# Adjacency of a graph network: 400 supersteps of four windows become 200 of eight over two PSUM banks

## The chip, the cores and the metric

The kernel runs on one core of a Trainium2 chip. The metric is the device time of one execution in microseconds (us), the median of several runs.

## The reference

Two graph networks, one after the other, over 3125 nodes and 100000 edges sorted by destination. Each is added to its input and followed by a layer norm. All message passing is a sum over the edges:

```
msg = x[src]
summed = segment_sum(msg, dst, num_segments=3125)
cnt = segment_sum(ones(E), dst, num_segments=3125)
aggr = summed / maximum(cnt, 1.0)[:, None]
out = aggr @ W_l + b_l + x @ W_r
```

The first network does this twice; the second does three layers of aggregation, each with a router that picks two of eight experts. As the edges never change, the kernel counts them once into a dense adjacency matrix in bf16 (how many edges go from source s to destination d) and later multiplies the node features by it.

## The kernel before

The program goes through these parts in order: keys of the edges (to about 124 us), the adjacency matrix (127 to 498 us), its layout into pieces in device memory, two passes of the first network, three layers with experts, and the final projection. Only the adjacency stage and the small tables before it are touched.

**Windows and steps.** A source is split as 25 tiles of 128; a destination belongs to a window of four (`W = 4`). A window of the matrix is therefore `WC = 100` columns on 128 partitions, and there are `NW = 800` of them. The edges come in 800 chunks of 125. A chunk and a window that it touches make a step; there are `T = 1600` steps in the order of the windows. A step is one matmul: a one-hot of the source's low part (125 edges x 128) times a one-hot of the place within the window (125 edges x 100) adds the step's counts to 100 columns of PSUM.

**Supersteps.** `G = 4` steps that follow each other form a superstep, with one PSUM bank. Its windows are at most three beyond its first one. TensorE first clears columns 100 to 399 with a matmul of zeros (L1210), then the first step writes columns 0 to 99 with `start=True`, and each of the other three adds at an offset from its register (L1214). The registers come from `w_rel`, a table of the offsets in the superstep. They are loaded for two batches at once (L1199): 24 registers for eight supersteps.

**Four engines in a chain.** VectorE makes the one-hots of 16 steps, a batch, in two instructions (L702), four batches ahead at most; it waits for `s_step`, which the last matmul of a superstep raises. ScalarE waits for `s_step`, copies the first window to the ring `first_w` of eight places (L1087) and the three others straight into the adjacency matrix (L1089), at an offset from a register. GpSimd adds the first window from the ring to the matrix (L558), because that window can have sums of the superstep before it; it waits for the wide copy (`s_wide`) and its own last add (`s_first`). ScalarE's narrow copy waits until the add of eight supersteps before is done, and TensorE's zeroing matmul until ScalarE has copied the superstep of eight before (L1209). GpSimd and ScalarE load 16 registers for 16 supersteps at a time (`RS`, L551 and L1079). The loops: a head of 64 steps with constant waits, then 24 turns of 64 steps each.

The tables `w_off` and `w_rel` are made by VectorE in three instructions (L688 to L690), after which the stage starts. At its end VectorE and ScalarE wait for the last add and start the layout (L356).

Of the kernel before, what the change touches and what calls it, by code (L numbers as in the profile page):

```python
# [11 lines left out]
EPE = mybir.EngineType.PE  # L12
# [4 lines left out]
P = 128  # L17
# [8 lines left out]
NW = S * P // W  # L26
WC = W * S
T = C + NW
G = 4
B16 = 16  # L30
RS = 16
NOH = 4
TP = 400
ABSENT_DST = 8000
# [42 lines left out]
def build(nc, x, src, dst, Wl0, bl0, Wr0, Wl1, bl1, Wr1, W_in, b_in, router_W, router_b, weak_W, weak_b,  # L77
          strong_W1, strong_b1, strong_W2, strong_b2, conf_W, conf_b, W_out, b_out, out):
    with ExitStack() as ctx:
# [3 lines left out]
        def sem(name):  # L83
            return ctx.enter_context(nc.semaphore(name))
# [4 lines left out]
        psum = ctx.enter_context(nc.psum_tensor("psum", [P, 8, 512], F32))  # L89
# [15 lines left out]
        def carve(shape, dt, rows=P):  # L105
            n = 1
            for k in shape:
                n *= k
            cols = n * (1 if dt == BF16 else 2)
            a = arena[0:rows, used[0]:used[0] + cols]  # L110
            used[0] += cols
            assert used[0] <= 103900, used[0]
            a = a if dt == BF16 else a.bitcast(dt)
            names = "abcd"[:len(shape)]
            if len(shape) > 1:
                a = a.rearrange(f"p ({' '.join(names)}) -> p {' '.join(names)}", **dict(zip(names[1:], shape[1:])))
            return a


        adj = carve([NW * WC], BF16)  # L120
        build_from = used[0]
        ones_b = carve([512], BF16)
        zeros_b = carve([512], BF16)
        iota2 = carve([P, 2], BF16)
        lo_of = carve([T], BF16, CE)
        loc_of = carve([T], BF16, CE)
        w_off = carve([T // G], I32, 1)
        w_rel = carve([T // G * (G - 1)], I32, 1)
        oh1 = carve([NOH, B16 // 2, P, 2], BF16, CE)
        wf = oh1[0:1].rearrange("p b n c z -> p (b n c z)")[:, 0:2 * T].bitcast(F32)  # L130
        first_w = carve([8, WC], BF16)
# [132 lines left out]
        s_wide = sem("new_windows_copied"); s_first = sem("first_window_added"); s_zero = sem("adjacency_zeroed")  # L264
# [54 lines left out]
        def blk(p, b):  # L319

            return (p - 2) * NB + b
# [210 lines left out]
        def _(pool):  # L532
# [17 lines left out]
            def adds(i):  # L550
                _, off = nc.values_load_multi_w_load_instructions(  # L551
                    w_off[0:1, bass.ds(i * RS, RS)], engines=(EPOOL,), min_val=0, max_val=(NW - G) * WC,
                    skip_runtime_bounds_check_because="a window's offset")
                for u in range(RS):
                    pool.wait_ge(s_wide, i * RS + u + 2)
                    pool.wait_ge(s_first, i * RS + u + 1)
                    a = adj[:, bass.ds(off[u], WC)]
                    pool.tensor_tensor(a, first_w[:, u % 8], a, ALU.add).then_inc(s_first, 1)  # L558
            with pool.Fori(0, T // G // RS) as i:
                adds(i)  # L560
# [12 lines left out]
            for l in range(NL):  # L573
                pool.memset(b1v[:, l, 0:NS, 2:FT], 0.0).then_inc(s_prep, 1)
            pool.wait_ge(s_first, T // G + 1)
            pool.wait_ge(s_wide, T // G + 1)
            pool.memset(x_all[:, S - 1], 0.0).then_inc(s_xpad, 1)
# [56 lines left out]
        def _(v):  # L634
# [3 lines left out]
            n = [0]  # L638

            def link(ins):  # L640
                n[0] += 1
                ins.then_inc(s_v, 1)
                v.wait_ge(s_v, n[0])
# [42 lines left out]
                v.nop().then_inc(s_gread, 1)  # L686
            w4 = wf[:, :].rearrange("o (s g) -> o s g", g=G)
            link(v.tensor_scalar(w_off[:, :], w4[:, :, 0], float(WC), None, ALU.mult))  # L688
            link(v.tensor_tensor(w_rel[:, :].rearrange("o (s g) -> o s g", g=G - 1), w4[:, :, 1:G], w4[:, :, 0:1].broadcast_to((1, T // G, G - 1)), ALU.subtract))
            v.tensor_scalar(w_rel[:, :], w_rel[:, :], float(WC), None, ALU.mult).then_inc(s_tab, 1)  # L690
            v.wait_ge(s_zero, 2)
            v.wait_ge(s_tab, 1)

            k = B16 // G
# [370 lines left out]
        def _(act):  # L1065
# [3 lines left out]
            for e in range(NE):  # L1069
                n = CAP // P  # L1070
# [7 lines left out]
            def supersteps(i, head=False):  # L1078
                _, off = nc.values_load_multi_w_load_instructions(  # L1079
                    w_off[0:1, bass.ds(i * RS, RS)], engines=(EACT,), min_val=0, max_val=(NW - G) * WC,  # L1080
                    skip_runtime_bounds_check_because="a window's offset")
                for u in range(RS):
                    act.wait_ge(s_step, i * RS + u + 1)
                    if not head or u >= 8:

                        act.wait_ge(s_first, i * RS + u - 6)
                    act.copy(first_w[:, u % 8], psum[:, u % 8, 0:WC])  # L1087
                    act.wait_ge(s_wide, i * RS + u + 1)
                    act.copy(adj[:, bass.ds(off[u] + WC, (G - 1) * WC)], psum[:, u % 8, WC:G * WC]).then_inc(s_wide, 1)  # L1089
            supersteps(0, head=True)  # L1090
            with act.Fori(1, T // G // RS) as i:
                supersteps(i)
# [55 lines left out]
            for p in range(2, 5):  # L1148
# [9 lines left out]
                for b in range(NB):  # L1158
                    i = blk(p, b)
# [14 lines left out]
        def _(pe):  # L1174
# [17 lines left out]
            k = B16 // G  # L1192
            def supersteps(i, head=False):


                for q in range(NOH):
                    if q % 2 == 0:
                        n = 2 * k * (G - 1)
                        _, rel = nc.values_load_multi_w_load_instructions(  # L1199
                            w_rel[0:1, bass.ds(i * (NOH // 2 * n) + q // 2 * n, n)], engines=(EPE,), min_val=0, max_val=(G - 1) * WC,  # L1200
                            skip_runtime_bounds_check_because="a window's offset in its superstep")
                    pe.wait_ge(s_oh1, i * NOH + q + 1)
                    pe.wait_ge(s_oh2, i * NOH + q + 1)
                    for g in range(k):
                        u = q * k + g
                        bank = psum[:, u % 8]

                        if not head or u >= 8:
                            pe.wait_ge(s_wide, i * (NOH * k) + u - 6)  # L1209
                        pe.matmul(bank[:, WC:G * WC], zeros_b[:, 0:P], zeros_b[:, WC:G * WC], start=True, stop=False, skip_group_check=True)  # L1210
                        for z in range(G):
                            cols = bass.ds(rel[(q % 2 * k + g) * (G - 1) + z - 1], WC) if z else slice(0, WC)
                            n = (g * G + z) // 2
                            mm = pe.matmul(bank[:, cols], oh1[:, q, n, :, z % 2], oh2[:, q, n, :, z % 2],  # L1214
                                           start=(z == 0), stop=(z == G - 1), skip_group_check=True)
                        mm.then_inc(s_step, 1)
            supersteps(0, head=True)
            with pe.Fori(1, T // B16 // NOH) as i:
                supersteps(i)
# [279 lines left out]
```

## Time and profile before

| | |
|---|---|
| median of 3 runs | 2634.7 us (2622.96 to 2635.31) |
| the profiled execution's own time | 2652.03 us |
| its span | 2650.4 us |
| TensorE matmuls busy | 2061.1 us (78%) |
| VectorE / ScalarE / GpSimd busy | 887.1 / 605.0 / 682.1 us |
| adjacency stage, first one-hot to last add | 127 to 498 us |

In the rows, PE is TensorE's matmuls and PEld its weight loads; DVE is VectorE, ACT ScalarE, POOL GpSimd. A name that ends in q (PEldq, POOLq) is the engine's sequencer, whose instructions (register loads, register arithmetic, branches) are not counted as busy. `[0.23 <-ACT ...]` behind a row is the idle time before it and what ended it. L12 is line 12 of the kernel.

### The profile page before, as it was taken

The page shows a single profiled execution, that of the slowest core. Times are in us where ns is not written, and L with a number is a line of the kernel's source. Part 1 is how long each engine was busy: PE and PEld are TensorE (multiplying, and loading weights), DVE is VectorE, ACT ScalarE, POOL GpSimd, SP SyncE. Part 2 cuts the span into 40 slices and gives each one's busy share as a digit, 9 for nine tenths or more (in the row PEclk, how much of TensorE's full clock was granted, in tenths as well). Part 3 has the DMA queues.
Part 4 walks back from the last instruction along what each step waited for, and adds up shares of the span by engine and source line. Part 5 has one row for each costly group of instructions (what it writes and reads, how often), then busy time and mean ns, then how long its engine had stood idle before and what let it go on. Part 6 is the DMA issues. An engine that isn't in the chain of part 4 may idle for free.

```text
span 2650.4 us, 37862 instructions
## 1 busy us (share of the span) xinstructions
PE 2061.1 (78%) x12490; PEld 1567.8 (59%) x12491; DVE 887.1 (33%) x2222; ACT 605.0 (23%) x1548; POOL 682.1 (26%) x821
## 2 busy tenths in 40 slices
PE   2666666239999898699958999699958999699953
PEld 1354444226667666577736776577736776577742
DVE  3476666333333322333332011332332011332334
ACT  0055656610011000223311000233211000233310
POOL 4177676300000033222210122222210122222210
PEclk9667676669999888799978989799978999799985
DMA  9400000495476653122256331122257331122232
GB/s 321 129 1 0 0 0 0 167 372 181 146 205 221 214 183 128 61 65 68 70 217 240 106 114 68 53 72 66 65 202 263 106 116 66 54 68 71 65 133 89
DMA packets 180467, 315.84 MB, mean 119 GB/s; under 512 B 48431, under 2 KB 138853, under 8 KB 180226
## 3 DMA queue, kind: packets, MB, share of 16 engines
q1 hardware_dynamic: 132210, 221.11, 25.4%
q0 software_dynamic: 21392, 65.09, 6.8%
q10 hardware_dynamic: 26752, 28.12, 3.2%
q8 instruction: 74, 1.21, 0.2%
q14 instruction: 39, 0.32, 0.0%
HBM read 198.96 MB, written 115.30 MB: 119 GB/s over the span
## 4 chain that ended last, share of the span: by engine, by line
PE 46%; DMA 16%; issue 13%; POOL 8%; DVE 8%; ACTq 3%; ACT 3%; SPq 1%; POOLq 1%; another core or an unknown queue 0%; DVEq 0%
PE psum L1314 14%; PE psum L1428 13%; DMA arena<-xs_d 10%; POOL arena L558 8%; PE psum L1228 7%; DMA arena<-h_d 4%; ACTq L1071 3%; PE psum L1406 2%; DVE arena L992 2%; PE psum L1391 1%; ACT arena L1089 1%; DMA adj_d<-arena 1%; DVE arena L994 1%; PE psum L1233 1%; PE psum L1417 1%
## 5 line engine op out<-in xcount | busy, mean ns | idle before, releaser
L1314 PE MATMUL psum<-arena 128*128 128x320 bf16 x3750 | 549.1, 310 | 89.0 <-DVE arena L1012 75.2
L1314 PEld LDWEIGHTS psum<-arena 128*128 128x128 bf16 x3750 | 376.9, 101 | 256.1 <-issue 98.3
L1417 PE MATMUL psum<-arena 128*128 128x256 f32 x1536 | 360.9, 389 | 2.1 <-ACT arena L1143 2.0
L619 POOL DMA_INDIRECT y_d<-arena,idx x192 | 202.3, 1054 | 605.0 <-DVE arena L994 596.3
L1428 PE MATMUL psum<-arena 128*128 x1536 | 352.5, 382 | 3.2 <-ACT arena L1146 3.2
L1417 PEld LDWEIGHTS psum<-arena 128*128 128x128 f32 x1536 | 281.3, 193 | 66.6 <-ACT arena L1146 18.6
L1428 PEld LDWEIGHTS psum<-arena 128*128 128x128 f32 x1536 | 284.1, 190 | 44.5 <-issue 6.4
L1146 ACT ACTIVATE arena<-psum,b1c 128x256 f32<-128x256 f32 x384 | 181.8, 473 | 494.0 <-PE psum L1417 493.5
L1228 PE MATMUL psum<-arena 128*128 128x320 bf16 x1500 | 225.1, 302 | 80.8 <-DMA arena<-adj_d 80.8
L558 POOL TENSOR_TENSOR arena<-arena 128x100 bf16 x400 | 257.1, 643 | 118.1 <-ACT arena L1089 64.2
L606 POOL DMA_INDIRECT xs_d<-arena,pos x150 | 144.6, 964 | 524.4 <-DVEq L849 483.3
L702 DVE TENSOR_TENSOR arena<-arena 125x1600 bf16<-125x1600 bf16 x200 | 232.5, 1207 | 120.3 <-PE psum L1214 120.2
L1210 PE MATMUL psum<-arena 128*128 128x300 bf16 x400 | 162.9, 407 | 135.9 <-DVE arena L702 74.3
L992 DVE TENSOR_TENSOR arena<-psum,arena 128x256 f32<-128x256 f32 x192 | 81.5, 425 | 528.2 <-PE psum L1428 528.2
L1228 PEld LDWEIGHTS psum<-arena 128*128 128x128 bf16 x1500 | 148.1, 99 | 139.2 <-DMA arena<-adj_d 81.0
L1214 PE MATMUL psum<-arena 125*128 125x100 bf16 x1600 | 204.5, 266 | 0.0
L1214 PEld LDWEIGHTS psum<-arena 125*128 125x128 bf16 x1600 | 171.3, 131 | 36.0
L1089 ACT CAST arena<-psum 128x300 f32 x400 | 166.0, 415 | 0.0
L1210 PEld LDWEIGHTS psum<-arena 128*128 128x128 bf16 x400 | 45.0, 112 | 164.4 <-ACT arena L1089 123.7
L1406 PE MATMUL psum<-ident,arena 128*128 128x128 f32 x384 | 64.1, 290 | 90.9 <-DMA arena<-xs_d 90.3
L1087 ACT CAST arena<-psum 128x100 bf16<-128x100 f32 x400 | 96.9, 242 | 160.6 <-POOL arena L558 112.1
L1116 ACT COPY arena<-psum 128x384 f32<-128x384 f32 (+1 forms) x50 | 19.1, 428 | 489.7 <-PE psum L1356 488.7
(238 smaller groups left out, 1572.8 us busy)
## 6 DMA issues: line engine op xcount, KB each, us to landing
arena<-adj_d SPq DMA_DIRECT2D x125, 800.0 KB, 6.3
xs_d<-zrow ACTq DMA_DIRECT2D x8, 3432.0 KB, 28.9
arena<-xs_d SPq DMA_DIRECT2D x96, 264.0 KB, 2.8
adj_d<-arena SPq DMA_DIRECT2D x25, 800.0 KB, 7.4
arena<-y_d SPq DMA_DIRECT2D x30, 640.0 KB, 6.1
arena<-h_d SPq DMA_DIRECT2D x25, 640.0 KB, 7.2
h_d<-arena POOLq DMA_DIRECT2D x15, 640.0 KB, 3.7
arena<-x_d SPq DMA_DIRECT2D x20, 320.0 KB, 3.7
```

The source lines that it names most:

```text
L558: pool.tensor_tensor(a, first_w[:, u % 8], a, ALU.add).then_inc(s_first, 1)
L606: pool.indirect_dma_start(xs_d, bass.IndirectOffsetOnAxis(ap=pos[:, k, t:t + 1], axis=0), pay[:, k, t], None).then_inc(a_scat, 16)
L619: pool.indirect_dma_start(y_d, bass.IndirectOffsetOnAxis(ap=idx[:, j % 2, h:h + 1], axis=0), ybuf[:, j % 2, h], None).then_inc(b_sc[j % 2] ...
L702: v.tensor_tensor(oh[:, q], every, key, ALU.is_equal).then_inc(ready, 1)
L1089: act.copy(adj[:, bass.ds(off[u] + WC, (G - 1) * WC)], psum[:, u % 8, WC:G * WC]).then_inc(s_wide, 1)
L1146: act.activation(hid[:, j % 2, f], psum[:, 5 + f % 2, 0:M], ACT.Relu, bias=b1c[:, bass.ds(at_b1[j % LOAD] + f, 1)]).then_inc(b_hidf, 1)
L1210: pe.matmul(bank[:, WC:G * WC], zeros_b[:, 0:P], zeros_b[:, WC:G * WC], start=True, stop=False, skip_group_check=True)
L1214: mm = pe.matmul(bank[:, cols], oh1[:, q, n, :, z % 2], oh2[:, q, n, :, z % 2], start=(z == 0), stop=(z == G - 1), skip_group_check=True)
L1228: mm = pe.matmul(psum[:, h, 0:HN], hs[:, k * SK + s, part, 0:P], half(ring[:, k, s], h), start=(k == 0 and s == 0 and part == 0), stop=(k ...
L1314: mm = pe.matmul(psum[:, q, 0:HN], hs[:, k * SK + s, part, f * P:(f + 1) * P], half(ring[:, k, s], h), start=(k == 0 and s == 0 and part = ...
L1417: mm = pe.matmul(psum[:, 5 + f % 2, 0:M], w1s[:, j % 2, f // 2, kt, f % 2 * P:(f % 2 + 1) * P], xsT[:, j % 2, kt], start=(kt == 0), stop=( ...
L1428: mm = pe.matmul(psum[:, h, 0:H], hid[:, j % 2, f, h * P:(h + 1) * P], w1f[:, bass.ds(at_w2 + f * H, H)], start=(f == 0), stop=(f == FT - 1))
```

## The change

`G` becomes 8: 200 supersteps of eight steps. Eight windows of 100 columns don't fit one bank of 512, so a superstep takes two banks that lie side by side: windows 0 to 4 in the first (`GA = 5`, 500 columns), 5 to 7 in the second. An offset from the sixth window on is raised by `PAD = 12` columns, which VectorE works into `w_rel` with two instructions more than a plain product needs. TensorE has two zeroing matmuls per superstep, of 400 and 300 columns, and the ring of PSUM is four pairs of banks instead of eight banks. The registers of the offsets are loaded once per superstep, seven at a time, behind the waits for the one-hots and ahead of the wait for ScalarE. ScalarE copies 100, 400 and 300 columns per superstep. `RS` becomes 8, so GpSimd and ScalarE load eight registers at a time. The ring `first_w` keeps eight places.

```diff
--- before.py
+++ after.py
@@ -26,9 +26,11 @@
 NW = S * P // W
 WC = W * S
 T = C + NW
-G = 4
+G = 8
 B16 = 16
-RS = 16
+RS = 8
+GA = 512 // WC
+PAD = 512 - GA * WC
 NOH = 4
 TP = 400
 ABSENT_DST = 8000
@@ -686,8 +688,10 @@
                 v.nop().then_inc(s_gread, 1)
             w4 = wf[:, :].rearrange("o (s g) -> o s g", g=G)
             link(v.tensor_scalar(w_off[:, :], w4[:, :, 0], float(WC), None, ALU.mult))
-            link(v.tensor_tensor(w_rel[:, :].rearrange("o (s g) -> o s g", g=G - 1), w4[:, :, 1:G], w4[:, :, 0:1].broadcast_to((1, T // G, G - 1)), ALU.subtract))
-            v.tensor_scalar(w_rel[:, :], w_rel[:, :], float(WC), None, ALU.mult).then_inc(s_tab, 1)
+            rel3 = w_rel[:, :].rearrange("o (s g) -> o s g", g=G - 1)
+            link(v.tensor_tensor(w4[:, :, 1:G], w4[:, :, 1:G], w4[:, :, 0:1].broadcast_to((1, T // G, G - 1)), ALU.subtract))
+            link(v.tensor_scalar(rel3, w4[:, :, 1:G], float(GA), float(PAD), ALU.is_ge, ALU.mult))
+            v.scalar_tensor_tensor(rel3, w4[:, :, 1:G], float(WC), rel3, ALU.mult, ALU.add).then_inc(s_tab, 1)
             v.wait_ge(s_zero, 2)
             v.wait_ge(s_tab, 1)
 
@@ -1084,9 +1088,10 @@
                     if not head or u >= 8:
 
                         act.wait_ge(s_first, i * RS + u - 6)
-                    act.copy(first_w[:, u % 8], psum[:, u % 8, 0:WC])
+                    act.copy(first_w[:, u % 8], psum[:, u % 4 * 2, 0:WC])
                     act.wait_ge(s_wide, i * RS + u + 1)
-                    act.copy(adj[:, bass.ds(off[u] + WC, (G - 1) * WC)], psum[:, u % 8, WC:G * WC]).then_inc(s_wide, 1)
+                    act.copy(adj[:, bass.ds(off[u] + WC, (GA - 1) * WC)], psum[:, u % 4 * 2, WC:GA * WC])
+                    act.copy(adj[:, bass.ds(off[u] + GA * WC, (G - GA) * WC)], psum[:, u % 4 * 2 + 1, 0:(G - GA) * WC]).then_inc(s_wide, 1)
             supersteps(0, head=True)
             with act.Fori(1, T // G // RS) as i:
                 supersteps(i)
@@ -1194,22 +1199,20 @@
 
 
                 for q in range(NOH):
-                    if q % 2 == 0:
-                        n = 2 * k * (G - 1)
-                        _, rel = nc.values_load_multi_w_load_instructions(
-                            w_rel[0:1, bass.ds(i * (NOH // 2 * n) + q // 2 * n, n)], engines=(EPE,), min_val=0, max_val=(G - 1) * WC,
-                            skip_runtime_bounds_check_because="a window's offset in its superstep")
                     pe.wait_ge(s_oh1, i * NOH + q + 1)
                     pe.wait_ge(s_oh2, i * NOH + q + 1)
                     for g in range(k):
                         u = q * k + g
-                        bank = psum[:, u % 8]
-
-                        if not head or u >= 8:
-                            pe.wait_ge(s_wide, i * (NOH * k) + u - 6)
-                        pe.matmul(bank[:, WC:G * WC], zeros_b[:, 0:P], zeros_b[:, WC:G * WC], start=True, stop=False, skip_group_check=True)
+                        bank = psum[:, u % 4 * 2:u % 4 * 2 + 2].rearrange("p b n -> p (b n)")
+                        _, rel = nc.values_load_multi_w_load_instructions(
+                            w_rel[0:1, bass.ds(i * (RS * (G - 1)) + u * (G - 1), G - 1)], engines=(EPE,), min_val=0, max_val=(G - 1) * WC + PAD,
+                            skip_runtime_bounds_check_because="a window's offset in its superstep")
+                        if not head or u >= 4:
+                            pe.wait_ge(s_wide, i * (NOH * k) + u - 2)
+                        pe.matmul(bank[:, WC:GA * WC], zeros_b[:, 0:P], zeros_b[:, WC:GA * WC], start=True, stop=False, skip_group_check=True)
+                        pe.matmul(bank[:, 512:512 + (G - GA) * WC], zeros_b[:, 0:P], zeros_b[:, 0:(G - GA) * WC], start=True, stop=False, skip_group_check=True)
                         for z in range(G):
-                            cols = bass.ds(rel[(q % 2 * k + g) * (G - 1) + z - 1], WC) if z else slice(0, WC)
+                            cols = bass.ds(rel[z - 1], WC) if z else slice(0, WC)
                             n = (g * G + z) // 2
                             mm = pe.matmul(bank[:, cols], oh1[:, q, n, :, z % 2], oh2[:, q, n, :, z % 2],
                                            start=(z == 0), stop=(z == G - 1), skip_group_check=True)
```

## Rows read from the trace of the kernel before

**Rows 1.** Stretch, length, busy (instructions) of PE, PEld, DVE, ACT, POOL; clock, DMA, GB/s.

```profile
127.00:498.30 371.30, 242.62 (x2000) 178.39 (x2000) 232.38 (x200) 221.11 (x800) 257.11 (x401) 0.68 0.00 0
```

**Rows 2.** The chain of work that ended last, stage alone, share by line.

```profile
by line: POOL arena L558 58.7%; issue 16.0%; ACT arena L1089 9.7%; POOLq L558 3.0%; POOLq L555 2.4%; ACT arena L1087 1.9%; DVE arena L702 1.7%; PE psum L1210 1.5%; PE psum L1214 1.5%; POOLq L556 1.4%; ACTq L1083 0.8%; POOLq L551 0.6%; ACTq 
```

**Rows 3.** Waits in the stage: us in total, times, longest.

```profile
DVE arena L702 <- PE psum L1214: 120.2, 87, 2.6
ACT arena L1087 <- POOL arena L558: 112.1, 167, 1.6
```

**Rows 4.** Groups of instructions in the stage: busy us, mean ns, idle before.

```profile
L558 POOL TENSOR_TENSOR arena<-arena 128x100 bf16 x400 | 257.1, 643 | 118.1 <-ACT arena L1089 64.2 <-POOL arena L558 53.9
L1089 ACT CAST arena<-psum 128x300 f32 x400 | 166.0, 415 | 0.0
```

**Rows 5.** Timeline: start us, us, engine, line; adds of GpSimd and VectorE's one-hots.

```profile
307.16 2.31 DVE L702 TENSOR_TENSOR arena<-arena 125x1600 bf16<-125x1600 bf16 x2 [0.33 <-PE psum L1214]
308.61 1.06 POOL L558 TENSOR_TENSOR arena<-arena 128x100 bf16 x1 [0.23 <-POOL arena L558]
310.50 0.35 POOL L558 TENSOR_TENSOR arena<-arena 128x100 bf16 x1 [0.23 <-POOL arena L558]
```

**Rows 6.** Register loads (one source line each): count, ns min/median/max, first and last start.

```profile
L1199 PEldq TENSOR_LOAD <-arena x50: 1613/1617/1802, 126.9 to 484.0; - x50
...
L341 ACTq TENSOR_LOAD <-arena x12: 545/549/774, 1074.0 to 2475.7; - x12
L341 PEldq TENSOR_LOAD <-arena x12: 588/598/1132, 1089.2 to 2482.4; - x12
```

**Rows 7.** Source line 1199 in short windows: its load or register work, start us.

```profile
L1199 PEldq TENSOR_LOAD <-arena x1: 1634/1634/1634, 132.8 to 132.8; - x1
...
L1199 PEldq TENSOR_LOAD <-arena x1: 1627/1627/1627, 138.1 to 138.1; - x1
...
L1199 PEldq FUSED_REGOPS  x1: 46/46/46, 144.0 to 144.0; - x1
```

**Rows 8.** TensorE's loop end (L1218) and register offsets of the steps (L1214).

```profile
L1218 PEldq FUSED_REGOPS  x24: 68/68/73, 137.9 to 477.4; - x24
L1218 PEldq COMPARE_BRANCH  x24: 76/208/242, 150.5 to 490.2; - x24
...
L1214 PEldq FUSED_REGOPS  x1200: 37/46/51, 129.0 to 490.0; - x172
```

**Rows 9.** Timeline of ScalarE: its two copies and the next superstep's first.

```profile
310.31 0.24 ACT L1087 CAST arena<-psum 128x100 bf16<-128x100 f32 x1
310.45 0.41 ACT L1089 CAST arena<-psum 128x300 f32 x1
310.89 0.24 ACT L1087 CAST arena<-psum 128x100 bf16<-128x100 f32 x1
```

**Rows 10.** Timeline of TensorE in the head: first and eighth superstep.

```profile
129.04 0.43 PE L1210 MATMUL psum<-arena 128*128 128x300 bf16 x1 [17.15 <-DVE arena L702]
...
133.10 0.45 PE L1210 MATMUL psum<-arena 128*128 128x300 bf16 x1
133.35 0.54 PE L1214 MATMUL psum<-arena 125*128 125x100 bf16 x4
```

**Rows 11.** Timeline of VectorE: the tables before the stage.

```profile
124.01 0.51 DVE L688 TENSOR_SCALAR arena<-arena 1x400 int32<-1x400 f32 x1
124.56 1.40 DVE L689 TENSOR_TENSOR arena<-arena 1x1200 int32<-1x1200 f32 x1
125.98 0.77 DVE L690 TENSOR_SCALAR arena<-arena 1x1200 int32<-1x1200 int32 x1
```

**Rows 12.** Timeline of the stage's end.

```profile
490.09 0.35 PE L1214 MATMUL psum<-arena 125*128 125x100 bf16 x4
...
497.94 0.35 POOL L558 TENSOR_TENSOR arena<-arena 128x100 bf16 x1 [0.23 <-POOL arena L558]
...
498.32 0.90 DVE L356 COPY arena<-arena 128x640 bf16<-128x640 bf16 x3 [18.69 <-POOL arena L558]
```

## The prediction

> **What bounds the kernel now.** I read first the busy times of the stretch that the diff touches, from the first one-hot at about 127 us to the last add of GpSimd at 498.3 us [rows 1]. In those 371.3 us no engine is full: GpSimd 257.1 us, TensorE 242.6, VectorE 232.4, ScalarE 221.1. DMA does nothing. So the stage is a loop of four engines that hand work to each other, and the busy shares alone don't name its bound. The chain of that stretch does [rows 2]: 58.7% of it is GpSimd's add at L558, 9.7% ScalarE's wide copy at L1089, and only 3.0% TensorE's matmuls L1210 and L1214. The waits say the same [rows 3]: ScalarE's narrow copy waits 112.1 us for L558 (its ring of eight `first_w` is full), and VectorE waits 120.2 us for TensorE, which itself stands behind ScalarE's copies. Everything backs up behind GpSimd.
>
> Why is GpSimd slow with 400 adds of 128x100? Its mean is 643 ns, but two levels make it [rows 4, 5]: 0.35 us when VectorE is idle, and 1.06 us while a one-hot of L702 runs. The add at 308.61 meets VectorE's pair of one-hots, which runs from 307.16 to 309.47, and takes 1.06 us; the one at 310.50 meets none and takes 0.35. With about 0.23 us between adds a free one costs 0.6 us and a covered one 1.3.
>
> Then the question that decides the forecast: who is next when GpSimd has half the adds? For that I read the sequencer of TensorE, which shows in no busy time. Its load of 24 registers takes 1617 ns in the median, 50 times [rows 6]. Between two loads it hands out eight supersteps. In the first turn of the loop the load begins at 138.1 and lasts 1.627 us, so it ends at 139.73; the register work of the next load is at 144.0 [rows 7]. That is 4.3 us for eight supersteps, and ScalarE was not holding TensorE there: the array's own pace in the head is 0.58 us per superstep [rows 10], and these eight took 0.54. So the sequencer today needs 2.15 us for 16 steps (half of 4.3) and 0.81 us for its half load, 2.96 in all, 296 us over the 100 batches; 24 loop ends with 68 + 208 ns [rows 8] make 7 more. 303 us of the 369 us from the first matmul to the last add: hidden behind GpSimd, but close.
>
> **The change part by part.** The unit is 16 steps (one batch of one-hots), 100 of them.
>
> GpSimd: 4 adds become 2, each still 128x100. At worst both are covered by VectorE: 2 x 1.3 = 2.6 us per batch, 260 us in all; uncovered 120 us. Its load of registers goes from 16 to 8 in each of 25 turns, to 0.55 us if it goes as ScalarE's of eight [rows 6], off the path from then on.
>
> ScalarE: today 0.58 us per superstep: 0.14 us from the narrow copy's start to the wide one's, 0.44 to the next narrow one [rows 9]. The 300 columns take 415 ns [rows 4] and the 100 take 242 [rows 9], 0.87 ns a column, so 400 columns take 0.50 us. After: 0.14 + 0.50 + 0.03 of issue, then 0.44 for the 300 columns, 1.1 us per superstep of eight steps, 2.2 us per batch, 220 us in all. Not a bound if anything needs more.
>
> VectorE: the one-hots are the same 200 instructions, 2.31 us for the pair of a batch [rows 5], 232 us in all [rows 1]. It waits on TensorE's steps with four batches of slack as before.
>
> TensorE's array: two zeroing matmuls of 400 and 300 columns for eight steps where two of 300 stood: 1500 columns against 1400. In this stage the records show a granted clock of 0.68 on average [rows 1], a mix of the 1.2 and the 2.4 GHz level. At the low one a superstep of 700 columns repeats every 0.58 us [rows 10], so 1500 columns need 1.25 us, 2.5 us per batch.
>
> TensorE's sequencer: this is where the change costs. Two loads of seven registers per batch take the place of half a load of 24. A load of eight on this engine takes 598 ns (12 records, from 588) and one of 24 takes 1617 [rows 6]; the line through them is 88 + 63.7 ns a register, so seven take 534 ns. Bounds: 534 by the line, 598 by the nearest row. I take 534, 1.07 us per batch against 0.81. Of the rest of the batch: two waits with a computed value fall away. In the head, where the waits are constants, eight supersteps take 3.67 us (134.43 to 138.1) against 4.3 in the loop [rows 7]; over the 12 waits of the two batches this is 0.052 us each, so -0.10 us. Seven register offsets per eight steps instead of six, at 46 ns [rows 8]: +0.09. Address work for 2 loads instead of 0.5, 46 ns each: +0.07. The number of matmuls and weight loads stays (2 zeroing and 8 steps for eight steps, before and after). Sum 2.15 - 0.10 + 0.09 + 0.07 + 1.07 = 3.28 us per batch: 328 us, with the 24 loop ends 335; the four batches of the head, with constant waits, take off 1: 334 us.
>
> Does the load lie beside the array's work? Yes: the load at 132.8 runs while the matmuls go on until 133.89 [rows 7, 10]. So the two times are not added; the larger decides, and 3.28 is over 2.5 (array), 2.3 (VectorE), 2.2 (ScalarE) and 2.6 (GpSimd). The new bound is TensorE's sequencer, with the nearest engine a fifth below, so little is lost by coupling.
>
> The PSUM ring is four supersteps of eight steps, 32 steps as before; ScalarE needs 1.1 us after a superstep and TensorE comes back to that pair of banks three supersteps, 4.9 us, later. The wait has lost none of its room. Queued behind it are that superstep's matmuls; its register load stands ahead of it.
>
> The table before the stage is on the path: L688, L689 and L690 take 0.51 + 1.40 + 0.77 us [rows 11], and L702 follows. After: 200 elements instead of 400 (0.3), a subtraction of 1400 instead of 1200 (1.64), a compare and multiply of 1400 (between 0.9 at L690's rate and 1.8 at L688's) and a last one of 1400 (1.64), with one more link. Together 4.6 to 5.5 us against 2.7 now; I take 2.3 more.
>
> The tail shrinks: today the last matmuls start at 490.09 and the last add at 497.94, because ScalarE and GpSimd are a ring behind [rows 12]. After, they keep up: 1.1 us of ScalarE, then 0.23 + 0.35 of an add and handing over, 2 us in all.
>
> **The sum.** First matmul now at 129.04 [rows 10], after at 131.3. Plus 334 is 465.3, plus 2 for the tail 467.3, and 1 us, a guess, for coupling: 468.3. Now it is 498.3. The layout copies start with that add [rows 12], and the DMAs, the x load and the aggregation hang on them in turn, so 30 us go through to the end. On the profiled execution's 2652.0 us this gives 2622. That execution is 17 us above the median of the runs shown (2634.7); 30 us off that median is 2605 us, 1.1% faster.
>
> A page speaks against small loads: the Trainium skill, "DMA: Bandwidth & Descriptors", section on latency and other measured facts, gives a register load from a tensor a floor of about 600 ns. The rows here show 549 ns on ScalarE and 598 on TensorE for eight [rows 6], so no firm floor at 600 shows; by it seven would cost 0.6 us, 13 us more over the 200 loads, and the time would be 2618, still inside the band that I give the forecast below.
>
> **The rivals.** (a) Nothing to be measured. The steady sequencer costs more than the one clean turn of the loop shows: the last turn needs about 4.6 us from its load's end (484.0 + 1.6) to its last matmuls at 490.1 [rows 6, 12], though ScalarE shares in that. With 2.3 us per batch and 598 ns a load: 3.28 + 0.15 + 0.13 = 3.56, 28 us more, 2633. (b) Slower. The array doesn't get work ahead of its sequencer while a load runs at the low clock, so that load and array add: 1.25 + 0.53 + 0.15 us of restart is 1.93 per superstep, 386 us for 200 and 7 for loop ends. Against 334 this is 59 us more: 2664. It turns from gain to loss at (369.3 - 2.3 - 2 - 1 - 7) / 200 = 1.78 us per superstep. Against it speaks the load at 132.8, which overlaps. (c) Much faster. If the sequencer holds the head's pace of 0.46 us per superstep in the loop, 1.84 + 1.07 + 0.15 = 3.06 us per batch, 22 us less: 2583. If register loads were hidden wholly, VectorE's and GpSimd's 2.6 us per batch would be next, 68 us less: 2537; nothing in the trace shows that: during the load from 132.8 to 134.43 the matmuls run out at 133.89 [rows 7, 10]. (d) The change doesn't do what it says, for instance because GpSimd's adds stay the bound: with half of them at most 260 us of work it can't.
>
> **How the numbers follow.** Forecast (2595 to 2620) 0.58; (a) 0.17; (b) 0.07; (c) at 2583 0.12 and at 2537 0.06, (d) nothing. The range leaves out (b) and the lower end of (c): 2572 to 2637. Half a percent, 13 us, is about what a measurement of this kernel can tell. Faster by more than that (below 2621.5): the forecast and (c), 0.76; within: (a), 0.17; slower: (b), 0.07.
>
> **What would show it.** The stage should run from about 131 to 468 us. GpSimd's 200 adds and ScalarE's waits on them vanish from the chain; the waits of TensorE for L1089 go too, and its idle time is put down to issue, or to nothing, beside 200 loads of about 534 ns. From one load to the next should be 1.64 us. If the stretch is GpSimd's again, or TensorE waits for VectorE, the step that names the next bound is wrong. If the loads take 600 ns or more, the price per register is. A superstep at 1.9 us would mean (b).

## The result and the profile after

The changed kernel takes 2835.0 us (2827.6 to 2839.1) against 2633.2 us of the kernel before, run along with it: 1.0757 times as long, 95% interval 1.0724 to 1.0791. The forecast was 2605 us. The change is 7.6% slower where 1.1% faster was forecast. Further down, a variant's time given without an interval is that of a single execution; beside it stands the median of the kernel before, of which 13 executions that ran together spread over 22 us.

The profiled execution of the changed kernel spans 2833.2 us. The granted clock in 40 slices of the span (tenths of full speed):

```profile
PEclk9655555555599999879998899979997989799985
```

The stage takes the slices from the second to the tenth, where TensorE's clock stays at the lower of its two levels, 1.2 GHz (0.50 in the next row). The same stretch as [rows 1], from the first one-hot to the last add (stretch, length, then busy time and instructions of PE, PEld, DVE, ACT, POOL, then the clock):

```profile
122.00:694.50 572.50, 285.65 (x2000) 186.68 (x2000) 212.63 (x202) 190.37 (x601) 164.89 (x205) 0.50 0.00 0
```

572.5 us where it was 371.3. GpSimd's work went from 257.1 to 164.9 us, ScalarE's from 221.1 to 190.4, VectorE's from 232.4 to 212.6. Only the matmuls grew, from 242.6 to 285.7 us, half of the stretch: eight steps have 1500 columns for 1400 before, and the granted clock fell from 0.68 to 0.50. Every engine is idle more than before, so something that isn't counted as busy fills the stretch. The chain of the stage, shares by line, which answers to [rows 2]:

```profile
by line: issue 26.5%; PE psum L1217 23.0%; PE psum L1212 17.3%; ACT arena L1094 11.8%; PE psum L1213 8.5%; DVE arena L706 4.5%; ACT arena L1093 2.7%; ACT arena L1091 1.8%; POOL arena L560 1.4%; ACTq L1094 1.3%; ACTq L1090 0.9%; DVEq L706 0.
```

GpSimd's add fell from 58.7% to 1.4%, as forecast, and TensorE's three lines hold 48.8%. But the waits, read by themselves, lead astray (engine, line, waited for, us in total, times, longest). The longest of TensorE's matmuls:

```profile
PE psum L1212 <- ACT arena L1094: 220.3, 149, 1.7
```

It puts 220.3 us of TensorE's idleness down to ScalarE's copy L1094. A stretch of the timeline shows that this isn't what ended it (start us, us, engine, line, idle before):

```profile
300.94 0.51 PE L1212 MATMUL psum<-arena 128*128 128x400 bf16 x1 [1.65 <-ACT arena L1094]
...
301.50 0.87 PE L1217 MATMUL psum<-arena 125*128 125x100 bf16 x8
...
302.93 0.43 ACT L1094 CAST arena<-psum 128x300 f32 x1
...
303.81 0.51 PE L1212 MATMUL psum<-arena 128*128 128x400 bf16 x1 [1.44 <-ACT arena L1094]
```

ScalarE's copy ends at 303.36, and TensorE goes on at 303.81. Besides, by the code TensorE waits for the copy of four supersteps before, not for this one. What ended the wait is in TensorE's sequencer. Its register loads (count, ns min/median/max, first and last start), first all, then those that begin at 293.8, 296.0 and 302.0 us:

```profile
L1207 PEldq TENSOR_LOAD <-arena x200: 1059/1699/1725, 124.5 to 689.4; - x100
...
L1207 PEldq TENSOR_LOAD <-arena x1: 1062/1062/1062, 293.8 to 293.8; - x1
...
L1207 PEldq TENSOR_LOAD <-arena x1: 1699/1699/1699, 296.0 to 296.0; - x1
...
L1207 PEldq TENSOR_LOAD <-arena x1: 1699/1699/1699, 302.0 to 302.0; - x1
```

The load from 302.0 takes 1.699 us and ends at 303.70, just ahead of the matmul at 303.81. The forecast named this as a sign of being wrong: loads of 600 ns or more. Seven registers take three times the 534 ns forecast, and longer than 24 did before [rows 6]. The records show two prices only: the first and the fifth load of each turn of eight supersteps take 1062 ns (that at 293.8 is one), the other six 1700. The mean of the 200 is 1.543 us.

### The profile page after: what moved, and what is told of

It is laid out like the page before. It is cut to its first block, busy times and chain, and to the rows that moved or that the text cites. A ratio compares the mean times of both kernels' runs of the same rounds, so it can differ in the third digit from the quotient of the medians.

```text
span 2833.2 us, 36773 instructions
## 1 busy us (share of the span) xinstructions
PE 2088.6 (74%) x12490; PEld 1572.4 (55%) x12491; DVE 867.4 (31%) x2223; ACT 574.3 (20%) x1348; POOL 590.9 (21%) x621
## 4 chain that ended last, share of the span: by engine, by line
PE 54%; DMA 15%; issue 13%; DVE 8%; ACT 4%; ACTq 3%; SPq 1%; POOL 1%; another core or an unknown queue 0%; DVEq 0%; POOLq 0%
PE psum L1317 15%; PE psum L1431 12%; DMA arena<-xs_d 9%; PE psum L1231 7%; PE psum L1217 5%; PE psum L1212 3%; DMA arena<-h_d 3%; ACTq L1075 3%; ACT arena L1094 2%; PE psum L1409 2%; PE psum L1394 2%; PE psum L1213 2%; DVE arena L996 1%; DMA adj_d<-arena 1%; PE psum L1236 1%
## 5 line engine op out<-in xcount | busy, mean ns | idle before, releaser
L1317 PEld LDWEIGHTS psum<-arena 128*128 128x128 bf16 x3750 | 375.1, 101 | 248.9 <-issue 93.9
L1212 PE MATMUL psum<-arena 128*128 128x400 bf16 x200 | 102.2, 511 | 301.7 <-ACT arena L1094 220.3
L706 DVE TENSOR_TENSOR arena<-arena 125x1600 bf16<-125x1600 bf16 x200 | 212.3, 1105 | 337.8 <-PE psum L1217 337.7
L560 POOL TENSOR_TENSOR arena<-arena 128x100 bf16 x200 | 164.6, 823 | 413.1 <-ACT arena L1094 412.9
L1231 PEld LDWEIGHTS psum<-arena 128*128 128x128 bf16 x1500 | 147.8, 99 | 132.9 <-DMA arena<-adj_d 75.1
L1212 PEld LDWEIGHTS psum<-arena 128*128 128x128 bf16 x200 | 20.8, 104 | 344.5 <-ACT arena L1094 289.9
L1217 PEld LDWEIGHTS psum<-arena 125*128 125x128 bf16 x1600 | 160.4, 146 | 56.4 <-issue 36.4
L1217 PE MATMUL psum<-arena 125*128 125x100 bf16 x1600 | 174.7, 284 | 0.0
L1091 ACT CAST arena<-psum 128x100 bf16<-128x100 f32 x200 | 48.5, 243 | 397.7 <-PE psum L1217 364.9
L1409 PEld LDWEIGHTS psum<-ident,arena 128*128 128x128 f32 x384 | 41.4, 143 | 129.7 <-DMA arena<-xs_d 67.4
```

What stands on the lines that cost most here:

```text
L706: v.tensor_tensor(oh[:, q], every, key, ALU.is_equal).then_inc(ready, 1)
L1212: pe.matmul(bank[:, WC:GA * WC], zeros_b[:, 0:P], zeros_b[:, WC:GA * WC], start=True, stop=False, skip_group_check=True)
L1231: mm = pe.matmul(psum[:, h, 0:HN], hs[:, k * SK + s, part, 0:P], half(ring[:, k, s], h), start=(k == 0 and s == 0 and part == 0), stop=(k ...
L1317: mm = pe.matmul(psum[:, q, 0:HN], hs[:, k * SK + s, part, f * P:(f + 1) * P], half(ring[:, k, s], h), start=(k == 0 and s == 0 and part = ...
L1409: mm = pe.transpose(psum[:, 4, f * M + h * P:f * M + (h + 1) * P], xsl[:, j % 2, h, f * P:(f + 1) * P], ident[:, :])
```

## The experiments

The first four change only what a load reads: how many registers and from which address. An offset table entry has 4 bytes. In the changed kernel the loads start 28 bytes apart, so the first and fifth of each eight start at a multiple of 16 bytes (0 and 112) and no other does. In the diffs the long call that loads registers is cut to the slice of the table that it reads. Where the offsets lie eight apart, room for them comes from a shorter array of zeros (400 columns instead of 512, which is all that the matmuls read) and 40 columns more in the arena.

**Eight registers, aligned.** The offsets of a superstep lie eight apart; the eighth is a zero that VectorE writes.

```diff
-        w_rel = carve([T // G * (G - 1)], I32, 1)
+        w_rel = carve([T], I32, 1)
-                            w_rel[0:1, bass.ds(i * (RS * (G - 1)) + u * (G - 1), G - 1)]
+                            w_rel[0:1, bass.ds(i * (RS * G) + u * G, G)]
```

> The changed kernel with eight registers per superstep instead of seven; a superstep's offsets lie eight apart in the table, so every load starts at a multiple of 32 bytes. The eighth is a zero that nobody uses. Theory A (address): a load that starts at a multiple of 16 bytes takes four registers in one access of about 255 ns (the slope from 8 to 24 registers in the kernel before), any other takes one access per register of about 230 ns. Then a load here takes 598 ns as the aligned eights of the kernel before, the period per superstep falls from 2.85 to 0.60 + 1.31 = 1.91 us, and the time from 2835 to 2835 - 200 x 0.94 = 2647 us. Theory B (place): the load is slow because it stands right behind ten matmuls and waits for something of theirs. Then it stays at 1.7 us and the time at 2835. Theory C (count): a count that isn't a multiple of four is slow, the address is free. Then 598 ns and 2647 us too.

Measured: 2644.9 us against 2630.0 of the kernel before, ratio 1.0051 (1.0027 to 1.0075). The loads:

```profile
L1208 PEldq TENSOR_LOAD <-arena x200: 587/592/775, 123.6 to 499.6; - x100
```

One register more and 1.1 us less. Against the kernel before, 15 us are left of 202, and theory B (the place behind the matmuls) is out: the load stands where it stood and takes a third. The kernel is still no faster than the one before; that comes up below.

**Seven registers, aligned.** The same table, but seven are loaded.

```diff
-                            w_rel[0:1, bass.ds(i * (RS * (G - 1)) + u * (G - 1), G - 1)]
+                            w_rel[0:1, bass.ds(i * (RS * G) + u * G, G - 1)]
```

> The changed kernel with its seven registers per superstep, but a superstep's offsets lie eight apart in the table, so each load starts at a multiple of 32 bytes. Theory A (address): all 200 loads take what the first and fifth of each loop turn take now, 1062 ns (one access for four registers, three single ones), so 200 x (1.540 - 1.062) = 96 us less: 2739 us. Theory B (place): 1.7 us, 2835. Theory C (count): seven is still not a multiple of four, 1.7 us, 2835 us.

```profile
L1207 PEldq TENSOR_LOAD <-arena x200: 1052/1062/1255, 130.9 to 600.5; - x100
```

2744.3 us against 2739 expected by the address, and every load has the price that only the first and the fifth had. The count matters too, then: from the same addresses seven take 470 ns longer than eight.

**Eight registers, the table one element later.**

```diff
-        w_rel = carve([T // G * (G - 1)], I32, 1)
+        w_rel = carve([T + 8], I32, 1)[:, 1:T + 1]
```

> Eight registers per superstep, eight apart, but the whole table is shifted by one element, so that no load starts at a multiple of 16 bytes. Theory A (address): eight single accesses, 88 + 8 x 230 = 1930 ns, 200 x 0.39 = 78 us more than the changed kernel: 2913 us. Theory B (place): 1.7 us, 2835. Theory C (count): 598 ns, 2647 us.

```profile
L1208 PEldq TENSOR_LOAD <-arena x200: 1931/1933/2131, 123.9 to 767.0; - x100
```

2901.8 us against 2913 expected. The same eight registers cost 1933 ns at an address of 4 bytes beyond a multiple of 16, 592 at the multiple. Theory C, the count alone, is out.

**The kernel before, its table one element later.**

```diff
-        w_rel = carve([T // G * (G - 1)], I32, 1)
+        w_rel = carve([T // G * (G - 1) + 8], I32, 1)[:, 1:T // G * (G - 1) + 1]
```

> The kernel before with nothing changed but the place of its table of offsets: one element later, so that its 50 loads of 24 registers don't start at a multiple of 16 bytes. Theory A (address): 24 single accesses, 88 + 24 x 230 = 5.6 us instead of 1.62; with 4.3 to 4.6 us for eight supersteps between loads TensorE's sequencer becomes the bound at about 10 us per eight supersteps, 500 us for the stage instead of 369, time about 2765 us. Theories B and C: loads of 1.62 us and 2633 us, as the kernel before.

```profile
L1199 PEldq TENSOR_LOAD <-arena x50: 5667/5671/5864, 126.7 to 633.7; - x50
```

A shift by four bytes alone costs the kernel before 155 us: 2785.3 against 2630.0, where 2765 was expected. Its loads of 24 registers go from 1.617 us [rows 6] to 5.671. Their starts are (633.7 - 126.7) / 49 = 10.35 us apart, so 4.67 us pass between two loads; 4.3 to 4.6 were expected, and this matters below. By the two shifted kernels a single register costs (5671 - 1933) / 16 = 234 ns on top of about 60; by the two aligned ones four registers cost (1617 - 592) / 4 = 256 ns on top of about 80. So a whole group of four at a multiple of 16 bytes costs what one register costs, and with it the prices of the changed kernel are worked out: 80 + 256 + 3 x 234 = 1038 ns (measured 1062) and 60 + 7 x 234 = 1698 (1700).

**The second half of the change alone: three registers per superstep, in supersteps of four.**

```diff
-                    if q % 2 == 0:
-                        n = 2 * k * (G - 1)
-                        _, rel = (w_rel[0:1, bass.ds(i * (NOH // 2 * n) + q // 2 * n, n)])
...
+                        _, rel = (w_rel[0:1, bass.ds(i * (RS * (G - 1)) + u * (G - 1), G - 1)])
```

> The second half of the change alone: supersteps of four as before, but each loads its own three registers behind the waits for the one-hots, as the change does with seven. By the prices found: three registers never fill an access of four, so each load takes 0.06 + 3 x 0.234 = 0.77 us at any address; with 0.17 us around it, 0.50 us of matmuls and offsets, 0.05 for the batch's waits and 0.04 for the loop's end this is 1.53 us per superstep, 610 us for 400 of them against the stage's 369: about 240 us slower than the kernel before of the same call. If small loads are cheap in supersteps of four, the loss belongs to the eights and their two banks instead, and the time stays within 1% of the kernel before.

```profile
L1202 PEldq TENSOR_LOAD <-arena x400: 762/766/963, 129.0 to 725.9; - x134
```

2842.4 us against 2610.3, 232 us more, and 766 ns a load as worked out. The small loads alone make a loss of this size, without supersteps of eight or a second bank. The 12 bytes from one load to the next put the starts at all four places within 16 bytes, and the time hardly differs (medians of 782 ns at a multiple of 16, 764 and 765 elsewhere): three registers never hold a group.

**The first half alone: supersteps of eight, registers in a heap.** One load of 28 for four supersteps; every load starts 112 bytes after the last, a multiple of 16, and holds seven whole groups.

```diff
+                    if q % 2 == 0:
+                        n = 2 * k * (G - 1)
+                        _, rel = (w_rel[0:1, bass.ds(i * (NOH // 2 * n) + q // 2 * n, n)])
...
-                        _, rel = (w_rel[0:1, bass.ds(i * (RS * (G - 1)) + u * (G - 1), G - 1)])
```

> The change with its supersteps of eight and its two banks, but with the registers loaded in a heap as the kernel before did: 28 for four supersteps, each load 112 bytes after the last and so at a multiple of 16. Theory A (address): a load takes 0.08 + 7 x 0.256 = 1.87 us, with 0.17 us of sequencer work around it 0.51 us per superstep; the rest is 0.98 us for the matmuls and their offsets, 0.10 for the batch's waits, 0.08 for the loop's end: 1.67 us per superstep, 334 us for the stage against 369 of the kernel before, 2595 to 2600 us. This is the number that the prediction gave for the change, so if it comes, the prediction's order of bounds was right and its price of a load was wrong. Rival: superstep size itself costs something that I don't see (coupling over four pairs of banks), then 2620 or more.

Measured: 2573.4 us against 2608.3, ratio 0.9867 (0.9840 to 0.9894). Its loads, the chain of the stage and the stage's busy times:

```profile
L1204 PEldq TENSOR_LOAD <-arena x50: 1872/1874/2063, 114.4 to 436.8; - x50
...
by line: PE psum L1219 27.2%; DVE arena L706 25.6%; issue 19.5%; PE psum L1214 15.4%; PE psum L1215 8.9%; ACT arena L1094 1.2%; DVEq L706 1.2%; DVEq L716 0.3%; DVEq L712 0.3%; ACT arena L1093 0.2%; ACT arena L1091 0.2%; ACTq L1094 0.1%; ACT
...
114.40:445.50 331.10, 231.01 (x2000) 171.91 (x2000) 228.35 (x201) 189.28 (x601) 183.54 (x201) 0.73 0.00 0
```

The time is 35 us below the kernel before, as expected; the 2595 to 2600 us were reckoned from a kernel before at 2633, which took 2608.3 here. The stage takes 331 us, 334 were expected, and GpSimd's add has no place among the lines of the chain. The forecast for the change was a ratio of 0.989. For a load of 28 the prediction's line gives 88 + 28 x 63.7 = 1872 ns, and 1874 was measured: among aligned loads of whole groups the line holds.

**The changed kernel without loads in the stage.** One load ahead of it; the offsets of all supersteps but the first, and with them the adjacency matrix, are left wrong.

```diff
-                        _, rel = (w_rel[0:1, bass.ds(i * (RS * (G - 1)) + u * (G - 1), G - 1)])
+            _, rel = (w_rel[0:1, 0:G - 1])
```

> The changed kernel with one load of seven registers ahead of the stage and none in it, so every superstep adds at the first one's offsets: the adjacency matrix is wrong, all instructions but the 200 loads stay. If the loads alone made the loss: TensorE's sequencer needs 1.16 us per superstep, so the next engine bounds, VectorE with 2.3 and GpSimd with up to 2.6 us per batch of two supersteps: a stage of 250 to 270 us, 2520 to 2545 us in all. If something else in the superstep of eight holds it, over 2600.

```profile
by line: DVE arena L706 75.1%; issue 19.6%; DVEq L706 2.2%; DVEq L716 1.6%; DVEq L712 0.8%; ACT arena L1094 0.4%; PE psum L1217 0.2%; PE psum L1212 0.1%; ACT arena L1093 0.1%; ACT arena L1091 0.1%; PE psum L1213 0.1%; ACTq L1096 0.0%; ACTq 
...
120.70:360.80 240.10, 155.73 (x2000) 119.27 (x2000) 236.58 (x201) 187.13 (x600) 187.89 (x201) 0.97 0.00 0
```

2478.5 us against 2608.3; 2520 to 2545 was expected. The stage is 240 us and belongs to VectorE: 236.6 us busy, 75.1% of the chain. It is below the 250 expected, since I had counted GpSimd as an equal neighbour, and it isn't: its adds take 187.9 us beside VectorE. So VectorE's one-hots set the floor of the stage for supersteps of eight. The heap's 331 us lie 91 above it, about what its 50 loads take (50 x 1.874 = 94 us).

**The kernel before without loads in the stage.** The same edit; the offsets of all supersteps but the first eight are wrong, and so is the matrix.

> The kernel before with its 50 loads of 24 registers replaced by one ahead of the stage; the offsets of all supersteps but the first eight are wrong, and with them the adjacency matrix. The prediction took GpSimd for the bound and the loads for hidden: then 2630 us, within 0.5%. Rival: the loads of 1.62 us stop TensorE so long that GpSimd runs dry behind them, and a part of 50 x 1.62 = 81 us is on the path: down to 2550.

Measured: 2608.1 us against 2608.3, ratio 0.9997 (0.9978 to 1.0016).

```profile
by line: POOL arena L558 60.3%; issue 15.8%; ACT arena L1089 10.5%; POOLq L558 3.2%; POOLq L555 2.5%; ACT arena L1087 2.1%; POOLq L556 1.4%; ACTq L1083 0.9%; PE psum L1213 0.7%; PE psum L1209 0.7%; POOLq L551 0.6%; DVE arena L702 0.4%; ACTq
...
119.90:489.00 369.10, 249.53 (x2000) 168.08 (x2000) 234.03 (x201) 221.14 (x801) 255.59 (x404) 0.62 0.00 0
```

GpSimd holds 60.3% of the chain, much as in [rows 2], and taking away 50 loads of 1.617 us brings nothing. The first step of the prediction stands: in the kernel before they were hidden, and GpSimd holds the chain with them and without.

**Supersteps of five.** 500 columns of one bank, batches of ten, 16 registers for four supersteps.

```diff
-G = 4
-B16 = 16
-RS = 16
+G = 5
+B16 = 10
+RS = 8
-                            n = (g * G + z) // 2
+                            n, odd = divmod(g * G + z, 2)
```

> The kernel before with supersteps of five windows (500 columns of one bank), batches of ten steps and loads of 16 registers for four supersteps, at multiples of 64 bytes. GpSimd has 320 adds instead of 400. By the sequencer's prices: a superstep 0.11 + 4 x 0.125 = 0.61 us, batch waits 0.10, load (1.10 + 0.17) / 4 = 0.32, loop end 0.65 / 8 = 0.08: 1.11 us, times 320 is 355 us against a stage of 369: 2616 us. Rival: GpSimd was the bound and nothing else, then 369 x 0.8 = 295 us and 2556.

Measured: 2583.3 us against 2608.3, ratio 0.9892 (0.9854 to 0.9929), a gain between the two expectations (25 us; 14 by the sequencer's prices, 369 - 355, and 74 by GpSimd's share).

```profile
L1199 PEldq TENSOR_LOAD <-arena x80: 1102/1107/1293, 126.6 to 467.4; - x80
...
126.50:473.30 346.80, 239.47 (x1920) 167.47 (x1920) 257.43 (x320) 203.06 (x640) 211.67 (x321) 0.70 0.00 0
```

The stage is 347 us, nearer to the sequencer's 355 than to GpSimd's 295. In its chain GpSimd's add has 1.6%, TensorE's two lines 37.5% and VectorE's one-hots 33.2%, so GpSimd had left the path here too. The one-hots in batches of ten cost VectorE 257 us instead of 232.

**The heap of 28 with two turns in one turn of TensorE's loop.**

```diff
-            with pe.Fori(1, T // B16 // NOH) as i:
-                supersteps(i)
+            with pe.Fori(1, (T // B16 // NOH + 1) // 2) as i:
+                supersteps(i * 2 - 1)
+                supersteps(i * 2)
```

> The kernel with 28 registers in a heap, with two turns of 64 steps in one turn of TensorE's loop, so that 12 loop ends go. In the trace of the changed kernel a loop end adds 0.65 us to TensorE's sequencer (branch of 0.21 us and what follows it) where the prediction had 0.28. If that is so and the sequencer still bounds the stage, 12 x 0.65 = 8 us fewer than the heap alone: a ratio to the kernel before of 0.984 against 0.987. If the longer body costs as much in fetching as the branch saves, 0.987 again.

Measured: 2567.2 us against 2610.3, ratio 0.9830 (0.9784 to 0.9877). It is the fastest kernel here that makes the right matrix, but its interval covers the heap's 0.9867, so the times don't show what the loop ends are worth. The stages of the two profiled executions are 331.1 and 327.4 us. The 0.65 us of the expectation was too much: it held the waits of the batch, which the records of the changed kernel's sequencer show at the other batch ends as well. From a load's end to the next load's start pass 1.39 us in the mean at those and 1.77 us at the loop's end, so a loop end adds 0.38 us and twelve of them 4.6.

## Why the prediction was wrong

**The bound before: right.** The kernel without loads, at 0.9997, shows that they weren't on the path, and with half the adds GpSimd left the chain. No run changes GpSimd's adds and nothing else.

**Who is next: right in the engine.** TensorE's sequencer became the bound: in the four kernels with one load per superstep of eight, 1.297 us pass in the mean from a load's end to the next one's start, whether the load takes 0.592, 1.063, 1.543 or 1.935 us. The heap kernel's stage of 331 us beside the sum's 334 is in part luck: its loads cost 0.470 us per superstep where the sum has 0.534, and the rest 1.176 where it has 1.136.

**The price of a load of seven: the step that failed.** The prediction drew a line through loads of 8 and 24 registers and read it at seven, 534 ns, with 598 ns as the other bound. Both rows came from loads that start at multiples of 16 bytes and hold whole groups of four, which nothing in the rows said; the line was taken as a price per register and is one per group. A load of seven, 28 bytes after the last, is another kind, and no row of the trace of before shows it. So 598 was no bound. Had a single register been priced like a group of four, as nothing excluded, the far end would have been 88 + 7 x 255 = 1870 ns. The measured mean is 1.543 us: 1.009 us more than forecast, 200 times, is 202 us.

The Trainium skill has the price of a single register: "Runtime: NRT & Kernel Launch", section on instruction fetch mechanics, gives about 200 ns a register even for many at once; it speaks of loads from device memory. The runs agree for unaligned tables in the core's own memory (234 ns), and differ where four lie at a multiple of 16 bytes (64 ns a register). By that page's figure seven registers would cost 1.4 us, an estimate; the time would then be 2605 + 200 x (1.4 - 0.534), near 2780 us, a rival that the prediction lacks (the change took 2835). It weighed only the floor of 600 ns of the Trainium skill, "DMA: Bandwidth & Descriptors", section on latency and other measured facts. A floor says nothing of how a load grows, and that decided here: 766 ns for three, 1699 for seven. Whether TensorE has a floor near 600 no run shows, since none loads less than two whole groups or three single registers; ScalarE's 549 ns [rows 6] lies below.

**The rest of a superstep: too low by 0.16 us.** The records of the sequencer give 1.297 us in the mean from a load's end to the next one's start, 1.136 were forecast (334 / 200 - 0.534): 32 us in all. About 17 of them, an estimate, are what a load brings around it. Against the heap's 1.18 us it is 0.12 us for three quarters of a load, so about 0.16 us of address work and hand-over per load; the kernel with three registers each against the shifted kernel before gives 0.16 as well (0.726 - 0.584 us for seven eighths of a load). The prediction had 0.046. Another 12 us come from the one clean turn of 4.3 us on which the forecast was built. With its loop ends that is 4.3 + 0.276 / 2 = 4.44 us between two loads, where the shifted kernel before, which the sequencer bounds, shows 4.67: 0.06 us per eight steps. That is what rival (a) warned of, with chance 0.17. So with the price of a load right and nothing else, the forecast would have been 2605 + 32 = 2637, no gain. The kernel with eight aligned registers bears this out: 200 x (0.592 + 1.297) = 378 us against 369.

**Overlap: right, and small.** The load from 302.0 begins while the group of matmuls from 301.50 still runs, to 302.37, so 0.37 us of the load's 1.70 lie beside the array, which then stands idle for 1.44. The sequencer does get ahead of the array, and rival (b) didn't happen: from the end of the load at 293.8 to the next at 296.0 it needs 1.15 us for a superstep on which the array is at work for 1.43 (300.94 to 302.37). The break-even of 1.78 us per superstep does hold: 1.89 us (eight aligned) loses 15 us, 1.65 us (the heap) gains 35, and the change is at 2.84.

**What would show it.** GpSimd left the chain as forecast. But TensorE's waits for ScalarE didn't go from the profile: 220.3 us stand under L1094 and not under issue, by the time of a semaphore that had long been met.

**The small terms.** The tables before the stage begin with L690, the one-hots with L706:

```profile
117.46 0.33 DVE L690 TENSOR_SCALAR arena<-arena 1x200 int32<-1x200 f32 x1
...
122.07 2.13 DVE L706 TENSOR_TENSOR arena<-arena 125x1600 bf16<-125x1600 bf16 x2
```

From L690 to L706 4.61 us against 2.84 before [rows 11], 1.8 more; 2.3 were forecast. The tail:

```profile
691.79 0.87 PE L1217 MATMUL psum<-arena 125*128 125x100 bf16 x8
...
693.82 0.35 POOL L560 TENSOR_TENSOR arena<-arena 128x100 bf16 x1 [2.50 <-ACT arena L1094]
```

The last add ends 1.5 us after the last matmul group, 2 were forecast, 8 before [rows 12].

**The balance** on the profiled executions: from the start of the tables to the last add 576.7 us, where the prediction had 344.3 (374.3 less 30): 232 us, of which loads 202 and the rest of the superstep 32. The part before the tables is 6.5 us shorter than before and the part behind the stage 13 us. These 20 us I have not traced; nothing in the diff touches these parts. The profiled execution of the kernel before was itself 17 us above its median, and in the kernels here the first one-hot starts anywhere from 114.4 to 128.5 us, so they are within what executions differ by. 2620 + 232 - 20 is about the measured span of 2833.

## What to carry to other kernels

Price a register load by its groups, not its registers: here whole groups of four from a multiple of 16 bytes cost a quarter to a third of what others did, per register. Lay tables out so that each load starts there and has a multiple of four, and load many at once, since each load also brings 0.16 us around it. Before reading a price off a line through two rows, ask what the two rows have in common that the new case lacks, and when all engines are idle for much of a stretch and a wait is put down to one that had long been done, look at the sequencer's own instructions.

## What the runs showed of the hardware

A load of registers from a table in the core's memory by TensorE's sequencer: 592 ns for 8, 1617 for 24 and 1874 for 28, all from multiples of 16 bytes; 766 for 3, 1062 for 7 from such a multiple, 1700 for 7, 1933 for 8 and 5671 for 24 from other addresses (3 cost nearly the same at either). The address of the first register decides for all: 24 from 4 bytes beyond a multiple of 16 span five whole groups that lie at one, and cost 24 single prices, 60 + 24 x 234 = 5676 ns. ScalarE's and GpSimd's sequencers were seen only with aligned eights and sixteens. Whether groups of four are the unit, or 16 bytes with elements of another size, wasn't tried.
